# Bump attention: the last key tile's hat function moves from VectorE to GpSimd, and the five engines' orders are made anew

## What is computed

```python
# z_k, z_q: one number per token and head; b_h: bandwidth of head h
# the reference sorts z and takes prefix sums; it computes, for each query i of head h:
#   out_i = sum_j max(0, 1 - |z_i - z_j| / b_h) * v_j          (j over the 512 keys)
bw = jax.nn.softplus(log_bw.astype(jnp.float32)) + BW_EPS
z_sort = jnp.take_along_axis(Zf, idx, axis=2)
out = sum_v_left * (1.0 - z_over) + sum_zv_left * inv_bw + sum_v_right * (1.0 + z_over) - sum_zv_right * inv_bw
ctx = ctx / jnp.asarray(T, ctx.dtype)
```

## Time and profile before

| | before |
|---|---|
| median of 3 runs | 1333.35 us (1330.24, 1333.35, 1344.09) |
| the profiled execution | 1328.69 us, of which the span of the trace is 1326.8 us |
| mean granted TensorE clock | 0.91 of full speed |
| busy: PE / PEld / DVE / ACT / POOL | 1126.8 / 646.6 / 775.0 / 614.6 / 351.6 us |

### The profile page before, as it was taken

One profiled execution on the slowest core, in us unless ns is written; L12 is line 12 of the kernel. 1 busy time (PEld: TensorE's weight loads), 2 busy tenths in 40 slices (PEclk: granted clock), 3 DMA queues, 4 the chain that ended last, 5 costly groups with the idle time before them and its releaser, 6 DMA issues.

```text
span 1326.8 us, 20038 instructions
## 1 busy us (share of the span) xinstructions
PE 1126.8 (85%) x7368; PEld 646.6 (49%) x7368; DVE 775.0 (58%) x2016; ACT 614.6 (46%) x1072; POOL 351.6 (26%) x743
## 2 busy tenths in 40 slices
PE   6949567879789999979988866879789999988996
PEld 5935332254344567744455432234344467764455
DVE  3654689974694411388346589984586331159544
ACT  2015246825247643316843535744327843323862
POOL 3041220234424200034504114025424400032520
PEclk9678758979899999989998967998879999999999
DMA  7032000031520000070024100022430000043011
GB/s 259 1 82 45 11 0 0 4 92 29 145 58 2 3 0 1 9 184 2 3 64 107 37 10 0 1 59 57 104 98 4 2 4 1 0 113 80 3 34 48
DMA packets 48791, 58.22 MB, mean 44 GB/s; under 512 B 16589, under 2 KB 41789, under 8 KB 48190
## 3 DMA queue, kind: packets, MB, share of 16 engines
q1 hardware_dynamic: 47830, 56.46, 16.0%
q10 hardware_dynamic: 864, 0.48, 0.1%
HBM read 35.26 MB, written 20.87 MB: 42 GB/s over the span
## 4 chain that ended last, share of the span: by engine, by line
PE 59%; DVE 23%; ACT 5%; issue 4%; DMA 4%; POOL 4%; SPq 1%; ACTq 0%; POOLq 0%; DVEq 0%
PE banks L1651 10%; PE banks L1661 10%; PE banks L1466 5%; PE banks L1454 5%; DVE sb_rmax L1596 5%; PE banks L1441 4%; ACT sb_arena L1317 2%; PE banks L476 2%; DVE sb_arena L1386 2%; PE banks L952 2%; POOL sb_rstd L467 2%; PE banks L471 2%; PE banks L942 2%; PE banks L1262 1%; DVE sb_st L448 1%
## 5 line engine op out<-in xcount | busy, mean ns | idle before, releaser
L1596 DVE TENSOR_REDUCE sb_rmax<-banks 128x1 f32<-128x512 f32 (+3 forms) x352 | 205.5, 637 | 64.8 <-PE banks L1443 64.0
L1525 ACT ACTIVATE sb_arena<-banks 128x512 f32<-128x512 f32 x320 | 173.2, 596 | 99.0 <-PE banks L1454 97.4
L1441 PE MATMUL banks<-sb_arena,sb_qs 128*128 128x512 bf16 (+3 forms) x512 | 130.2, 325 | 36.2 <-DVE sb_rmax L1596 19.2
L466 POOL TENSOR_SCALAR sb_var<-sb_mv 128x4 f32<-128x4 f32 x40 | 10.2, 255 | 546.5 <-DVE sb_mv L451 546.5
L1661 PEld LDWEIGHTS banks<-sb_w,sb_arena 128*128 128x128 f32 x1024 | 127.8, 192 | 41.6 <-issue 38.3
L1554 POOL TENSOR_SCALAR_AFFINE_SELECT sb_arena<-sb_arena 128x256 f32<-128x256 f32 x256 | 98.0, 407 | 171.3 <-ACT sb_arena L1525 170.9
L1716 ACT ACTIVATE sb_arena<-banks,sb_b 128x512 f32<-128x512 f32 x128 | 84.0, 685 | 126.9 <-PE banks L1651 126.4
L1775 DVE SCALAR_TENSOR_TENSOR sb_xall<-banks,sb_region,sb_xall 128x128 f32<-128x128 f32 x160 | 44.5, 344 | 162.8 <-PE banks L1661 162.8
L1317 ACT ACTIVATE sb_arena<-banks,sb_negmax 128x512 f32<-128x512 f32 x192 | 115.1, 715 | 44.9 <-PE banks L1262 30.0
L1661 PE MATMUL banks<-sb_w,sb_arena 128*128 128x128 f32 x1024 | 129.3, 275 | 1.6 <-ACT sb_arena L1716 1.5
L1651 PE MATMUL banks<-sb_ft,sb_w 128*128 128x512 f32 x256 | 128.0, 604 | 0.0
(11 more groups left out here) (290 smaller groups left out, 1912.5 us busy)
## 6 DMA issues: line engine op xcount, KB each, us to landing
sb_qs<-q_scratch SPq DMA_DIRECT2D x32, 288.0 KB, 4.9
q_scratch<-sb_region SPq DMA_DIRECT2D x16, 384.0 KB, 2.6
sb_arena<-k_scratch SPq DMA_DIRECT2D x16, 288.0 KB, 7.0
sb_arena<-in_chosen SPq DMA_DIRECT2D x8, 514.0 KB, 4.0
sb_w<-in_w SPq DMA_DIRECT2D x2, 2048.0 KB
q_scratch<-sb_region SPq DMA_DIRECT2D x16, 256.0 KB, 2.2
sb_qs<-q_scratch SPq DMA_DIRECT2D x32, 96.0 KB, 2.4
k_scratch<-sb_region SPq DMA_DIRECT2D x8, 384.0 KB, 2.7
```

The lines of the kernel that those rows point to most:

```text
L1441: nc.tensor.matmul(o[:, i * kl:(i + 1) * kl], L.qs[:, h // 2, t * 128:kl], L.ks[:, key_of(h), 0:kl], start=(i == 0), stop=False)
L1525: nc.scalar.activation(L.probs[:, u % SLOTS, :], bank_of(SELF_ORDER, ring, ("key", u)), ACT.Exp)\
L1596: nc.vector.tensor_reduce(L.rmax[:, t, g * GROUP + h0:g * GROUP + h0 + nh], bank_of(SELF_ORDER, ring, ("max", step))[:, 0:nh * kl] .rearra ...
```

## The change

The hat function of key tile 3 (the tile that comes from `differences`) is done by GpSimd in a TENSOR_SCALAR of 128x512, one per head, 64 in all; VectorE's TENSOR_SCALAR shrinks from 128x2048 to 128x1536. GpSimd's instruction waits for the reduction (`hat` 2h + 1) and signals a new semaphore `cut`; `weighted_values` waits for `cut` as well as for `hat` 2h + 2. VectorE's instruction no longer waits for its own reduction, since it doesn't touch tile 3. In `bump_pool` the 16 new instructions of a stage stand behind the masks and before `norm_pool`. The order numbers of all five engines are new.

```diff
@@ COUNTS @@
-           "filled": 1, "masks": 1, "spread": H, "raw": H, "dist": H, "hat": 2 * H, "pv": H, "osb": G, "y": 1, "res": 1},
+           "filled": 1, "masks": 1, "spread": H, "raw": H, "dist": H, "hat": 2 * H, "cut": H, "pv": H, "osb": G, "y": 1, "res": 1},
@@ ORDER @@
     "POOL":
-    "43f1b1caaf43c2efef294535fb26c58e5b41d7a2b76f4f72d0a4010007c5f796e4e6e6f5b4096cb4ec3f6f472cb94800001f"
+    "43f1c9cbfaca5cc05b16c4bf24fcae23df8cbf5a864b97553347fd931cd000004dce3ffe3a44fcabc950e0fa7924efad0d3d"
...
@@ bump_tensor, weighted_values @@
                 pe.wait_ge(*p.at("hat", 2 * h + 2))
+                pe.wait_ge(*p.at("cut", h + 1))
@@ bump_pool @@
             nc.gpsimd.tensor_scalar(L.mask[:], L.mask1, 0.0, None, ALU.is_equal).then_inc(L.sem("masks"), 1)
+            for h in range(H):
+                yield
+                pool.wait_ge(*p.at("hat", 2 * h + 1))
+                nc.gpsimd.tensor_scalar(L.dist[h % 3][:, 3, :], L.dist[h % 3][:, 3, :], bw[:, 1, h:h + 1],
+                                        bw[:, 1, h:h + 1], ALU.min, ALU.subtract).then_inc(L.sem("cut"), 1)
             yield from norm_pool(pool, L, p)
@@ bump_vector @@
                 dve.wait_ge(*p.at("dist", h + 1))
-                dve.wait_ge(*p.at("hat", 2 * h + 1))
-                nc.vector.tensor_scalar(L.dist[h % 3], L.dist[h % 3], bw[:, 1, h:h + 1], bw[:, 1, h:h + 1],
-                                        ALU.min, ALU.subtract).then_inc(L.sem("hat"), 1)
+                nc.vector.tensor_scalar(L.dist[h % 3][:, 0:3, :], L.dist[h % 3][:, 0:3, :], bw[:, 1, h:h + 1],
+                                        bw[:, 1, h:h + 1], ALU.min, ALU.subtract).then_inc(L.sem("hat"), 1)
```

More of the change, by code:

```diff
@@ L173 @@
     "SP":
-    "dd2c16d37fc10553fc016cbf806667fe482a1bdf821c1fe015c3fc05a650",
+    "9b92a6c9dfb02591fe016cbf406667fe242937b7121a3ee01aafcc0566608",
     "PE":
[L176 to L179, removed]
@@ L180 @@
-    "7e479c7fdef6b1080000000400b0ff75efc180dbb5cfd36e9bc70f8e726b9f073753e7667db3a9c39dc8800004028019157d"
-    "52afa3ca9b26b90c899e1b8237c0a81b5fbffc093cf3d1b6baf2acc9fa5a4b3b71595dbdf18797f4ac94f709000004100005"
-    "f6fcb415088303a8",
+    "a0adc179ccfff3af7505aaec7796d7dbaadcfe9f3650000000008bafb7ffddcac1ab15ca2b86a0001c1fdfdbffff9ee20288"
+    "92cce3fe7ffbfa10000008080087ecbfff240776cb9e75f96b68bb4b29b356d237ceef47ce7717786d420000081204a44af4"
+    "73d246cf73d09d7990545d983c04a236bbffb288b9dd73accf99f1a3e55173cdeb25c9f9afd8d97cba633904000020200017"
@@ L183 @@
+    "edf4b00d83eebfbffffffe93ad74e2f7ceffc420000400200200015fd7aff7cfe3b56688da60090100feacfffc7ffd987e11"
+    "15a55d1ffbfce908000002108200feeaffc102f6dc775ead2f964fb312e8d57b5dc2ebf65cf5cad15dc810000084406244fa"
+    "53b512c4f9c066ebdd29ae976804340b5efffc2227dc9d5f79936b68fa6e19d5d1f45ad7eb9d5d7632ac1f21000008100003"
+    "f5fb98e1004515064",
     "ACT":
-    "17932eea8f6be51d39feded3800002ebb72ec5624666ae983efd656f6dfac00081deb3b43b9c1b6a43cab64cb5753b5b7d79"
-    "9001020b469b15654a76c5a15314fdb8ebafba03c599ace9dacdd9fc6e300080107bc03b9ffcdbeaf78dd37c00208008f67b"
@@ L186 @@
-    "597508bad975dafc9659edeb9800002562f56fad3c534d8e8a6665d9b673e7afd0c0080c1a4e23b52b9198c6a2ab163ddc9f"
-    "36bc38d572a379cf3376fcc1d0010021eea00",
+    "e13336bb36d1fe5e2b75d7dc8000146ebf51a66900fcd74effda42373ebf400022a15bb6be7371e07706b4d873ab9e7adf5c"
+    "a0008409d32315de5caa45a155f92f3cf92e652c369ab2b5f2ad7975ed900080047ec01f5e1fe9fff35f4bec00400050fabd"
+    "736a40fa337a7ac92fdb473eb600030be2cd735883ee195c596ac8fae96bd3bdd940040903ae291c7495d3ca81ef68cf76aa"
+    "e91a174d66e1d6dab6dbdcc350020041f6c800",
@@ L188 @@
     "POOL":
-    "43f1b1caaf43c2efef294535fb26c58e5b41d7a2b76f4f72d0a4010007c5f796e4e6e6f5b4096cb4ec3f6f472cb94800001f"
-    "318ba27e8743bf3cf2f928eb48ea0ee2be52c6bf5b9baf11400100377667f2356f279947987e2ae239fab797c1100000540",
+    "43f1c9cbfaca5cc05b16c4bf24fcae23df8cbf5a864b97553347fd931cd000004dce3ffe3a44fcabc950e0fa7924efad0d3d"
+    "2c00001f198de3eee4d44ac293437e3bc30b9ee9bcbc4e235cb3b16e7ea2f442f004003ebbb8aae0ef79823f99964b8b7dcb"
+    "9fd90920000050",
     "DVE":
-    "038eb39067f47f7ad8bec355136499093fa8d527a7b6fc5a4d4c66a491905ce7de9cde447414e670fea9661a0037cbfbfa12"
@@ L193 @@
-    "162aac74cad28001fc866177b617cbffdb5412c92ab295ab10007f807ece87ffed5fbe2c59fd850a2c00511caaee3db7c9a2"
-    "d6b114641a81bf9ed55ea2c1e5507b9310b18d083df4fef25203c6ab8966b18002fc16c34bfa1797ffbc126d22ccca53acc0"
-    "007f813f900",
+    "0cc4d7903f6a7edf992bb0b5b14a54c7543ac9a7abe7fbc298317495828057cbeeaefa93394809d919c2da7300b7a7eff828"
+    "964b2ce2c6d30002fc16a52dde87a6fff43c46c52aa9596a84007fc03f8d87ff775fbfd5be11850e0420321ccb763f5beb59"
+    "4d4191280d923fb7d13f0729c60c4351d8a82eb037f1ff7084e2ab193566a94002fc865553fa872f7ffe00cf098f29597580"
@@ L196 @@
+    "007f807d3600",
 }
```

## The result

| | before | after |
|---|---|---|
| median, run beside each other on one chip | 1337.67 us (1330.24 to 1344.09) | 1357.21 us (1355.25 to 1361.67) |
| ratio, 95% interval | | 1.0167 (1.0115 to 1.0219) |
| profiled execution, span | 1328.69, 1326.8 us | 1355.47, 1353.6 us |
| both BU regions, first reduction to residual | 102.1 + 103.7 us | 116.2 + 121.3 us |

A forecast was written before the change was run, and what follows sets the result against it. VectorE was taken to set the pace in bump attention's middle windows at 2.06 us per head. 1328.7 + 48 (38 middle, 10 outer) = 1377 us; median forecast 1380, range 1325 to 1408, own mechanism 1367 to 1395.

The forecast's parts named there:

- The sum: Whole kernel: +38 us in middle windows and +10 us in outer windows, 1328.7 + 48 = 1377 us.
- The durations: Per head in bump attention: GpSimd's new 512-column instruction takes 2.06 us, VectorE's shrunken one 1.08 us.
- whole instructions in turn: Per head, GpSimd and VectorE shut each other out, holding the shared access 1.08 + 2.06 = 3.14 us.
- the other signs: Profile after: VectorE's instruction mean near 2.5 us or more, its busy sum up, GpSimd's up over 130 us.
- middle windows: Dense stretches of bump attention where both lanes' heads alternate: 35 heads x (3.14 - 2.06) = +38 us.
- outer windows: Four less dense windows of bump attention, 29 heads: 91 + 45.2 us GpSimd work against 126.7, +10 us (0 to +26).
- Rival 2: GpSimd works at the one-operation rate, 1.49 us, so 2.57 us per head: 1347 to 1359 us; chance 0.14.
- Rival 3: The engines do not shut each other out; GpSimd alone paces heads at 2.06 us: 1325 to 1340; chance 0.05.
- Rival 1: GpSimd is cheap, 0.61 us at the lower bound, and the change is faster: 1315 to 1329 us; chance 0.14.
- The regions: Both bump attention regions grow by 20 to 30 us each; the rest of the kernel equal within 8 us.
- The order at nothing: Rearranged instruction streams outside bump attention: taken as 0, with 8 us to either side.
- Rival 4: TensorE's clock falls in bump attention: 0.5 us per head, +15 to +30 on the sum, 1395 to 1410; chance 0.10.

The follow-up runs named there:

- collision kernel: A kernel of its own, computing nothing of the reference: in 122 trials GpSimd does one of six instructions beside VectorE's 1,536-column hat function at varied delays; no kernel ratio.
- quarter_cut: The changed kernel with GpSimd taking 256 of a head's 2,048 columns, VectorE 1,792 and waiting for its reduction again: 1341.90 us, ratio 1.0055 to the kernel before.
- late_small: order_only with two more 2-column GpSimd instructions ahead of GpSimd's 2-column one: 1351.22 us, ratio 1.0110 to the kernel before.
- order_only: The changed kernel with GpSimd keeping only 2 of a head's columns, VectorE 2,046 and waiting for its reduction again: 1327.87 us, ratio 0.9945 to the kernel before.
- small_cut: The changed kernel with GpSimd's part narrowed to 64 columns, the other 448 left as distances: 1307.53 us, ratio 0.9846 to the kernel before.
- small_hat: The changed kernel with VectorE's hat function narrowed to 64 of 1,536 columns, the rest left as distances: 1329.44 us, ratio 0.9958 to the kernel before.
- one_op_cut: The changed kernel with GpSimd doing only the min, the subtraction left out in tile 3: 1344.03 us, ratio 1.0076 to the kernel before.

## Why the prediction was right, and where it was not

The time (1357.21 us) and the side (slower) came as forecast: within the range of 1325 to 1408, and slower had 0.77 of the chances. But it lies outside the 1367 to 1395 that the forecast's own mechanism gave; the wide range holds it through its rivals. The sum was too large (48 us, where the span grew by 26.8), and one of its steps was wrong in kind.

- **The durations were right, one of them with luck.** GpSimd's two-operation 512 columns: 2.06 predicted, 2.062 the least measured. The line through the earlier trace rows was off at both of its parts and the two errors cancelled at 512: it has 0.442 us at 64 columns and 3.62 ns per column, where this instruction, with its scalars from memory, takes 0.568 us and 3.3 ns. VectorE's 1,536 columns: 1.08 predicted, 1.061 least and 1.071 median. The Trainium skill's 769 ns for 512 elements ("GPSIMD Engine Reference", "3.1 Elementwise — side-by-side cycle accounting") and its 1.8 cycles per element don't hold for this instruction here, and the measurement decides: 1.555 us with one operation, 2.062 with two.
- **The step that failed: whole instructions in turn.** I had put "So per head the pair holds that access for 1.08 + 2.06 = 3.14 us", from the collisions of the earlier trace rows and from the Trainium skill, "SBUF — State Buffer", "SBUF: two separate sides", which says that the two engines take turns as whole instructions. The collision kernel agrees for GpSimd's MEMSET, COPY, TENSOR_TENSOR and affine select (VectorE ends 0.81 to 0.82 us after each). The 3.80 us of the earlier trace rows were mostly the MEMSET of the earlier trace rows: of the 2.46 us that L1386 lost, 0.92 lie beside L1334 and 1.54 beside the MEMSET. Nor did they fit "to the tenth of a microsecond": L1386 ended at 203.08, 1.08 us after the MEMSET and not 1.34. TENSOR_SCALAR with a scalar from memory, the instruction of the change, doesn't hold VectorE off to its end: one that comes 0.5 to 1.3 us behind takes its 1.07 us. The row of L1333 showed only that GpSimd waits for VectorE, which is true in both cases; I read the other direction out of a row that had a MEMSET in it. So the heads overlap: 2.57 us in the middle, not 3.1 to 3.3.
- **What this did to the other signs.** L1392's mean of "2.5 us or more" is 1.217, and VectorE's busy sum went down by 9.1 us, not up. GpSimd's went up by 152.8 (over 130 predicted). It is mostly GpSimd that waits inside its instructions (0.44 us over its least on average), not VectorE (0.16 us). TensorE's wait does name GpSimd.
- **The term as it should have been.** With 2.57 us per head the middle windows give 35 x (2.57 - 2.06) = +18 us, rather less with the 2.32 of the second region. The outer windows, 29 x 2.57 + 45.2 = 120 us against 126.7, give nothing as a matter of work. The regions still grew by 14.1 and 17.6 = 31.7 us, since in the outer windows too the part is late for the product; my sum of work per engine has no place for that. quarter_cut shows such a loss outside the dense stretch; late_small, with 2 columns and GpSimd's time of 2.07 us per head, goes to 1.0110 from order_only's 0.9945.
- **Rival 2** gave 1347 to 1359, and the 1357.21 lies in it. Its number was near by chance: it had 2.57 us per head as 1.08 + 1.49 with whole turns and a faster GpSimd. The real 2.57 are the full 2.06 plus 0.5 of stretching. **Rival 3** is what happened in kind ("GpSimd alone paces the heads"), with "a small gap" that is 0.5 us. Its number, 1325 to 1340, was too low, and its premise, no shutting out at all, doesn't hold either. **Rival 1** put the best case of a cheap GpSimd at 1315: small_cut, freed of the order's 7 us, is at that (1307.5 + 7).
- **The regions** were to grow by 20 to 30 us each, and grew by 14.1 and 17.6. The rest was to stay within 8 us, and did: it has 5.5 more, and the first region starts 10.4 us sooner.
- **The order at nothing, 8 us to either side:** it is worth -0.55% (-0.1 to -1.0%), some 7 us.
- **Rival 4, the clock,** came in the second region alone. There the granted clock fell from 0.90 before to 0.77, and TensorE was busy 89.8 us instead of 77.7 for nearly the same instructions (461 and 463). The four kernels whose GpSimd part takes 2.07 us per head or more in all heads have 0.76 to 0.78 there, the others 0.84 to 0.88. In the first region it stayed (0.85 after, 0.83 before). A stretch of the second region, and one of the kernel before, show what a low clock does:

```profile
848.00:864.00 16.00, 9.54 (x60) 1.67 (x61) 10.30 (x12) 9.22 (x16) 16.00 (x8) 0.82 0.00 1
864.00:880.00 16.00, 16.00 (x71) 8.34 (x71) 5.69 (x14) 6.18 (x11) 7.80 (x5) 0.53 0.00 1
...
840.00:856.00 16.00, 14.01 (x106) 4.11 (x98) 15.78 (x19) 14.05 (x24) 0.00 (x0) 1.00 0.01 2
```

The first two rows are the change. TensorE is busy 9.54 of 16 us, and then, nearly all of the time at the lower level of 1.2 GHz (0.53), 16.00 of 16 us with 71 matmuls; the kernel before (third row) makes 106 in 14.01 us at the upper level (2.4 GHz), though not all of the same kinds. From 864 to 880 us TensorE, and neither GpSimd nor VectorE, is the busy engine. What the clock costs in all isn't separated by a run. Against order_only the second region grew by more than the first by 7.1 us in small_hat, 6.1 in one_op_cut, 1.7 in late_small and 0.7 in the change, but by 4.0 in quarter_cut too, whose clock was 0.84.

In ratios: order -0.55% (0.45 to either side), relief of VectorE -1.0%, GpSimd's part +3.2%, together +1.67%; the three add up by the way they are formed, each as a difference of two measured ratios with intervals of 0.4 to 0.5% to either side.

What stays open: the old order together with GpSimd's part wasn't tried, so the order's gain is measured only with a small part on GpSimd. No run keeps GpSimd busy behind its part without making the part late, so how much of the 3.2% is lateness and how much is GpSimd's own pace isn't known. Nor is the share of the clock.

## What to carry to other kernels

Before work goes to an idle engine, follow the result to its consumer: a part that ends later than the part it was split from delays everything that stands behind the join in an in-order stream, even if the new engine is the less busy one (quarter_cut: 149.5 against 175.5 us in both regions, 1.0055). Then look at the densest stretch by itself: there the new engine can be busy without a pause although its mean is low. A collision in a trace is evidence for the instruction in that very row, and for the direction in which it shows the wait. And when a change mixes a new split with a new order, run the order alone: here it was the part worth keeping (0.9945).

## What the runs showed of the hardware

- GpSimd's TENSOR_SCALAR with scalars from memory, float32 to float32, two operations: 0.363 us for 2 columns, 0.568 for 64, 0.786 for 128, 1.212 for 256, 2.062 for 512, at the least. That is 0.36 us and 3.3 ns per column. One operation: 1.555 us for 512.
- With two operations and 512 columns it delays a VectorE TENSOR_SCALAR that starts 0.1 to 0.5 us behind it, lets one that starts 0.5 to 1.3 us behind run its 1.07 us, and ends 0.46 us after that one. A TENSOR_TENSOR of 512 columns (1.26 us), a COPY (0.61 us), a MEMSET of 2,048 (1.80 us) and an affine select of 256 (0.40 us) hold VectorE off to their end: it ends 0.81 to 0.82 us after them.
- The earlier start doesn't settle who goes first. GpSimd's COPY, MEMSET, TENSOR_TENSOR and affine select went first though VectorE had started 0.03 to 0.05 us sooner; with the two-operation TENSOR_SCALAR VectorE went first from 0.03 us behind.
- When GpSimd loses, it waits for VectorE's instruction to end, except for about its own first 0.2 to 0.3 us. A 2-column instruction of GpSimd takes 0.37 us alone and 1.43 beside VectorE's 2,046 columns, as these rows of order_only's GpSimd timeline show:

```profile
210.68 0.37 POOL L1342 TENSOR_SCALAR sb_arena<-sb_arena,sb_bw 128x2 f32<-128x2 f32 x1 [0.44 <-DVE sb_arena L1390]
211.28 1.43 POOL L1342 TENSOR_SCALAR sb_arena<-sb_arena,sb_bw 128x2 f32<-128x2 f32 x1 [0.23 <-DVE sb_arena L1390]
```

Its mean over 64 heads is 1.00 us. So a GpSimd instruction that follows VectorE's reduction, with VectorE's next TENSOR_SCALAR right behind, costs about 1 us in this kernel even with 2 columns.
